# Block-diagonal keys moved by transfers, paired statistics and a 128-row routing product in a fused two-layer attention and feed-forward kernel

## The reference

```python
x = x + tanh(g_xattn[0]) * L0_xattn(layernorm(x), ctx, ctx)      # 32 query heads of 8, 8 key heads
x = x + tanh(g_ffn[0]) * L0_ffn(layernorm(x), ...)               # quantised gated block, hidden 704
x = x + tanh(g_xattn[1]) * L1_xattn(layernorm(x), ctx, ctx)      # 16 query heads of 16, 4 key heads
x = x + tanh(g_ffn[1]) * L1_ffn(layernorm(x), ...)               # 32 experts, the 8 best of each token
```

## Time and profile before

| | us |
|---|---|
| runs shown: median (lowest, highest) | 442.41 (442.10, 442.42) |
| profiled execution, device time | 442.06 |
| its span, first to last instruction | 440.3 |
| TensorE granted clock, mean | 0.984 of full |
| busy: PE / DVE / ACT / POOL | 391.7 / 301.8 / 223.9 / 216.4 |

### The profile page before, as it was taken

The page is one execution under the profiler, slowest core; times in us unless marked ns, Lnnn a source line. Parts: engine busy times, 40 slices in busy tenths (PEclk is TensorE's granted clock), DMA queues, the critical chain, the costliest instruction groups (busy, mean ns, idle before and its releaser), DMA issues.

```text
span 440.3 us, 6773 instructions
## 1 busy us (share of the span) xinstructions
PE 391.7 (89%) x2248; PEld 333.2 (76%) x2248; DVE 301.8 (69%) x603; ACT 223.9 (51%) x446; POOL 216.4 (49%) x234
## 2 busy tenths in 40 slices
PE   0697879897987988979999999999999999999994
PEld 0486778797986987957788887887687777788773
DVE  5486768878766877657678776665867665666664
ACT  2586766575556653535565544444454444444431
POOL 6788976643166533236666253544343344443510
PEclk9998989999999999969999999999999999999999
DMA  5921111000000000031321212223232343333101
GB/s 162 206 71 39 36 37 37 0 2 2 0 1 1 1 2 0 7 102 38 106 63 47 71 44 66 74 71 96 69 88 77 102 122 107 83 97 89 57 0 48
DMA packets 14339, 25.58 MB, mean 58 GB/s; under 512 B 4513, under 2 KB 7201, under 8 KB 14305
## 3 DMA queue, kind: packets, MB, share of 16 engines
q1 hardware_dynamic: 14304, 25.15, 20.1%
HBM read 24.10 MB, written 1.05 MB: 57 GB/s over the span
## 4 chain that ended last, share of the span: by engine, by line
PE 51%; DVE 3%; ACT 1%; issue 1%; DVEq 0%; ACTq 0%
PE bank L1250 15%; PE bank L1252 14%; PE bank L1251 14%; PE bank L1337 2%; PE bank L1149 1%; PE bank L1130 1%; PE bank L1172 1%; PE bank L1110 1%; DVE h_t L980 1%; PE bank L1205 1%; PE bank L1327 0%; ACT ot L623 0%; DVE hl L985 0%; DVE t_t L974 0%; DVE t_t L961 0%
## 5 line engine op out<-in xcount | busy, mean ns | idle before, releaser
L523 POOL TENSOR_TENSOR wl<-wraw,wh 128x768 fp32r<-128x768 f32 x48 | 88.7, 1848 | 109.3 <-DVE hl L985 109.3
L1250 PE MATMUL bank<-xh,wh 128*128 128x512 f32 (+1 forms) x288 | 109.2, 379 | 3.5 <-DVE t_t L961 3.5
L1252 PE MATMUL bank<-xh,wl 128*128 128x512 f32 (+1 forms) x288 | 103.3, 359 | 0.0
L1251 PE MATMUL bank<-xl,wh 128*128 128x512 f32 (+1 forms) x288 | 103.1, 358 | 0.0
L623 ACT ACTIVATE hh<-h_t 128x512 fp32r<-128x512 f32 (+1 forms) x72 | 40.3, 559 | 100.3 <-DVE h_t L980 83.0
L985 DVE TENSOR_TENSOR hl<-h_t,hh 128x512 fp32r<-128x512 f32 (+1 forms) x72 | 49.1, 682 | 24.8 <-ACT hh L623 24.7
L1250 PEld LDWEIGHTS bank<-xh,wh 128*128 128x128 f32 x288 | 55.2, 192 | 11.6 <-issue 3.2
L1252 PEld LDWEIGHTS bank<-xh,wl 128*128 128x128 f32 x288 | 55.0, 191 | 8.1
L961 DVE SCALAR_TENSOR_TENSOR t_t<-s_t,bank 128x512 f32<-128x512 f32 (+1 forms) x72 | 42.9, 595 | 26.3 <-ACT s_t L768 25.9
L1250 PE MATMUL bank<-hh,wh 128*128 128x512 f32 (+1 forms) x144 | 53.2, 370 | 8.4 <-DVE x L996 5.6
L1251 PEld LDWEIGHTS bank<-xl,wh 128*128 128x128 f32 x288 | 55.3, 192 | 7.0
(11 more groups left out here) (105 smaller groups left out, 616.0 us busy)
## 6 DMA issues: line engine op xcount, KB each, us to landing
wraw<-w SPq DMA_DIRECT2D x54, 384.0 KB, 3.1
out<-x SPq DMA_DIRECT2D x8, 128.0 KB, 2.4
x<-x_in SPq DMA_DIRECT2D x1, 768.0 KB, 5.0
ctx_v<-ctx_in SPq DMA_DIRECT2D x2, 256.0 KB, 7.0
ctx_k<-ctx_t SPq DMA_DIRECT2D x2, 192.0 KB, 3.3
x<-x_in SPq DMA_DIRECT2D x1, 256.0 KB, 2.7
wc<-wc_t SPq DMA_DIRECT2D x1, 256.0 KB, 3.9
ot<-sel_in SPq DMA_DIRECT2D x1, 256.0 KB, 5.3
```

What stands on the lines that cost most here:

```text
L523: ops.tensor_tensor(wl[:, slot, :], src, wh[:, slot, :].bitcast(F32), ALU.subtract).then_inc(F.w_split, 1)
L1250: nc.tensor.matmul(o, wh[:, slot, w_sl], rh, start=first, stop=False, skip_group_check=reopened)
L1251: nc.tensor.matmul(o, wh[:, slot, w_sl], rl, start=False, stop=False, skip_group_check=reopened)
L1252: return nc.tensor.matmul(o, wl[:, slot, w_sl], rh, start=False, stop=stop, skip_group_check=reopened)
```

## The change

1. **Keys.** For tiles 3 to 7 of each layer POOL makes no `kbd`. SP copies the diagonal blocks from `khl` (high and low part in one tile) into a slot whose zeros are there already: 16 transfers a tile in layer 0 (8 heads, two halves of the rows; 8 rows by 1 KB each), 8 in layer 1 (16 rows by 1 KB), written in runs of 256 bytes. `kbd`'s two middle dimensions change places for this. SP waits for `kh`, `kl` and the scores of the tile that leaves the slot; PE's `scores` waits for the transfers. In SP's queue a tile's transfers stand ahead of load(3) to load(7); layer 1's tiles 3 to 6 ahead of load(9), its tile 7 ahead of load(20).
2. **Statistics.** In layer 0, `ln_stats` and `power` take tiles in pairs, in the tick u = 1 of each even tile, in place of one tile in each.
3. **Routing.** `sel` and `wts` have 128 rows; rows 64 to 127 are zero (`sel` by its input, 512 KB in place of 256 KB; `wts` by a memset on POOL in step 4, for which `route_high` waits).

```diff
+WHOLE = 3
+def moved(layer, t):
+    at = [k for k in range(WHOLE, TT) if k % RING == t % RING]
+    if layer == 0:
+        return 16 * 16 * (at.index(t) + 1)
+    slot = (TT + t) % RING
+    below = [k for k in range(WHOLE, TT) if k % RING == slot]
+    return 16 * 16 * len(below) + 16 * 8 * (at.index(t) + 1)
...
+        khl = sb("khl", [P, BATCH, 2, KEYS], F32R)
+        kh, kl = khl[:, :, 0], khl[:, :, 1]
...
-        sel_raw = ot[0:2 * EXPERTS].rearrange("p k n -> p (k n)")
-        sel = sb("sel", [2 * EXPERTS, QUADS * P], F32R)
-        wts = sb("wts", [2 * EXPERTS, 2, BLK], F32R)
+        sel_raw = ot[:].rearrange("p k n -> p (k n)")
+        sel = sb("sel", [P, QUADS * P], F32R)
+        wts = sb("wts", [P, 2, BLK], F32R)
...
+            def move_keys(a, t):
+                sp.wait_ge(kh_ready, 2)
+                sp.wait_ge(kl_ready, 3)
+                sp.wait_ge(a.scored, a.units * (t - RING + 1))
+                slot = (a.layer * TT + t) % RING
+                for h in range(a.hk):
+                    for c in range(2):
+                        row = slice(64 * c + h * a.d, 64 * c + (h + 1) * a.d)
+                        sp.dma_start(kbd[row, slot, :, :, h * KEYS:(h + 1) * KEYS]...,
+                                     khl[row, 2 * t:2 * t + 2]...).then_inc(k_moved[slot], 16)
...
+                if WHOLE <= i < TT:
+                    move_keys(A[0], i)
+                if i == F0 + WRAW:
+                    for t in range(WHOLE, TT - 1):
+                        move_keys(A[1], t)
+                if i == 20:
+                    move_keys(A[1], TT - 1)
                 load(i)
...
             def key_part(a, t, r):
+                if t >= WHOLE:
+                    return
...
+                if u == 1 and t % 2 == 0 and t + 2 < TT:
+                    power(a, t + 2, t + 4)
                 if u == 1 and t + 2 < TT:
-                    power(a, t + 2, t + 3)
-                    if n == 9:
-                        pool.wait_ge(kl_ready, 3)
                     key_part(a, t + 2, 1)
...
+                if s == 4:
+                    ops.memset(wts[:].bitcast(F32), 0.0).then_inc(R.wt_zero, 1)
...
-                if u == 1 and t + 2 < TT:
+                if u == 1 and t % 2 == 0 and t + 2 < TT:
...
-                    ln_stats(a, t + 2, t + 3)
+                    ln_stats(a, t + 2, t + 4)
...
-                    if a.layer == 0:
+                    if t >= WHOLE:
+                        pe.wait_ge(k_moved[(a.layer * TT + t) % RING], moved(a.layer, t))
+                    elif a.layer == 0:
```

More of the change, by code:

```diff
@@ L290, in __init__ @@
         self.wt_lo = sem("r_wt_lo")
+        self.wt_zero = sem("r_wt_zero")
         self.sel_loaded = sem("r_sel_loaded")
@@ L315, in build @@
         ctx_k = sb("ctx_k", [P, BATCH, KEYS])
-        kh = sb("kh", [P, BATCH, KEYS], F32R)
-        kl = sb("kl", [P, BATCH, KEYS])
+        khl = sb("khl", [P, BATCH, 2, KEYS], F32R)
+        kh, kl = khl[:, :, 0], khl[:, :, 1]
         ctx_v = sb("ctx_v", [P, BATCH, 64])
@@ L392, in build @@
         kl_ready = sem("kl_ready")
+        k_moved = [sem(f"k_moved{i}") for i in range(RING)]
         v_zeroed = [sem("v_zeroed0"), sem("v_zeroed1")]
@@ L406, in keys @@
             shape = [P, 2, a.hk, KEYS]
-            part = kh[:].bitcast(F32) if r == 0 else kl[:]
+            part = khl[:, :, r].bitcast(F32)
             slot = (a.layer * TT + t) % RING
-            return ops.tensor_tensor(kbd[:, slot, r, :, 0:a.ns].rearrange("p b (h t) -> p b h t", t=KEYS),
+            return ops.tensor_tensor(kbd[:, slot, :, r, 0:a.ns].rearrange("p b (h t) -> p b h t", t=KEYS),
                                      part[:, b, :].unsqueeze(2).to_broadcast(shape),
@@ L437, in _ @@
                              ).then_inc(v_loaded, 16)
+            def move_keys(a, t):
[6 more added lines that the diff above has]
+                        row = slice(64 * c + h * a.d, 64 * c + (h + 1) * a.d)
+                        sp.dma_start(kbd[row, slot, :, :, h * KEYS:(h + 1) * KEYS].rearrange("p b r t -> p (b r) t").bitcast(F32),
+                                     khl[row, 2 * t:2 * t + 2].rearrange("p b r t -> p (b r) t").bitcast(F32)
+                                     ).then_inc(k_moved[slot], 16)
             def load(i):
@@ L799, in route_high @@
                 act.wait_ge(R.wt_done, h + 1)
+                act.wait_ge(R.wt_zero, 1)
                 copy(wts[0:EXPERTS, h, :], bank[PB][0:EXPERTS, :]).then_inc(R.wt_hi, 1)
@@ L1111, in scores @@
                                                 qt[:, t % 2, b2, 2 * gp:2 * gp + 2, :].rearrange("p g s -> p (g s)"),
-                                                kbd[:, slot, r, b2, 0:a.ns], start=(r == 0), stop=(r == 1))
+                                                kbd[:, slot, b2, r, 0:a.ns], start=(r == 0), stop=(r == 1))
                 done.then_inc(a.scored, 1)
@@ L1418 @@
         "kmask1": own_rows(4),
-        "sel_in": np.tile(np.repeat(np.eye(EXPERTS, dtype=np.float32), 32, axis=1), (2, 1)),
+        "sel_in": np.pad(np.tile(np.repeat(np.eye(EXPERTS, dtype=np.float32), 32, axis=1), (2, 1)),
+                         ((0, P - 2 * EXPERTS), (0, 0))),
     }
```

## The result

The changed kernel takes 436.84 us (median of 7 runs, 435.9 to 440.8) against 442.12 for the kernel before: ratio 0.9896 with a 95% interval of 0.9857 to 0.9935, so about 4.6 us faster. Forecast were 428.0 and a range from 422.5 to 435.5. The profiled execution took 436.58 us, its span is 434.5.

The account below looks back on a forecast made before the run. POOL's queue was taken to bound layer 0's attention and PE the experts' stage. 442.06 - 8.8 (keys) - 5.9 (routing) gave 427.4, 427.7 against the median, and 428.0 with 0.3 for layer 1's tile 7; range 422.5 to 435.5 us.

Parts of the forecast that it names:

- What takes POOL's place: SP: SP's queue with the key transfers: 0.6 us an issue, 9.6 us a tile, costing nothing, at most 1 us.
- part 1: Keys moved off POOL in layer 0's attention: 8.8 us gained, with ends of 3 and 11 us.
- Part 3: Routing product padded to 128 rows in the experts' stage: 5.9 us gained on PE, with ends of 0 and 6.4.
- deciding point of 1.1 us: Price per issue on SP up to which tile 3's 16 transfers in layer 0 still arrive before its scores.
- ACT waits for weight blocks 3 to 5: A sign that the prediction is wrong: ACT standing still for these blocks, which SP loads; no size given.
- POOL bounds layer 0's attention: POOL's queue makes its addition to x late there; 4.6 us of PE's idle time come from it.
- slow DVE instruction of 2.10 us: At 82.00 us, beside a POOL key product, where others of its size take 0.43; 1.3 us counted as gained.
- Part 2: Paired statistics in layer 0: some 2 us less on POOL, but no change of the time, within 0.3 us.
- Layer 1's tile 7: Its key transfers stand behind load(19) and end at 249.0, scores at 249.43; 0.3 us of cost allowed.
- SP becomes the bound: Rival: layer 0's 80 transfers make the kernel slower, 452 us at 1.3 us an issue, 500 at 1.9; chance 0.08.
- both effects cancel: Rival: gain and SP's cost balance with issues near 1.15 us, so the time does not change; chance 0.02.
- DVE and ACT as next bound: Rival: these engines hold layer 0's ticks, the moved keys give only 3 us, time 433.5 us; chance 0.14.
- a spread that costs the same: Rival: the routing product costs as much with 128 rows as with 64, time 434 us; chance 0.08.

Follow-up runs that it names:

- e9: The changed kernel with 13 in place of 16 key transfers for each tile of layer 0: 430.92 us, ratio 0.9735 to the kernel before.
- e4: The changed kernel with the routing product back at 64 rows: 443.56 us, ratio 0.9984 to the kernel before.
- e3: The kernel before with the paired statistics alone: 440.89 us, ratio 0.9944.
- e5: The changed kernel with loads ahead of layer 0's key transfers and the routing product at 64 rows: 435.75 us, ratio 0.9831 to the kernel before.
- e8: The changed kernel with POOL making tiles 3 and 4 of both layers and transfers from tile 5 on: 434.03 us, ratio 0.9829 to the kernel before.
- e1: The changed kernel with load(3) to load(7) ahead of layer 0's key transfers in SP's queue: 431.46 us, ratio 0.9744 to the kernel before.
- e6: The changed kernel with loads ahead of layer 0's key transfers and statistics of single tiles: 430.75 us, ratio 0.9721 to the kernel before.
- e2: The kernel before with the 128-row routing product alone: 438.17 us, ratio 0.9895.
- e7: The changed kernel with loads first and 16 more, unused transfers behind each tile's 16 in layer 0: 470.04 us, ratio 1.0603 to the kernel before.

## Why the prediction was wrong

**The step that failed** is "What takes POOL's place: SP", with its "Cost: nothing, with an upper end of 1 us". Its term was mis-sized: 0.60 us an issue, taken from transfers of 64 rows, where the 8-row ones take 0.73. In the sum that is 16 x 0.13 = 2.1 us a tile, and the loads stand behind up to three tiles of it: load(5) came at 62.43 in place of about 56. e9 gives the prediction its own price and lands at 0.9735 against the forecast's 428.0 / 442.4 = 0.967; the rest, 2.9 us, is about what parts 1 and 3 fell short by. The price lay well inside the bounds that I gave it (0.43 to 1.9), but I followed the upper end to the keys alone: tile 3's deadline, hence a deciding point of 1.1 us. load(4) and load(5) are behind the same transfers, and their deadlines moved nearer with the very ticks that part 1 shortens. ACT's timeline in the kernel before has the old deadline of block 5:
```profile
66.67 0.84 ACT L704 ACTIVATE wf<-wraw 128x768 f32<-128x768 int32 x1
```
In the changed kernel block 5 is there at 66.00, in time for the old pace; in e9 ACT takes it at 59.20. So whatever ticks 8 to 15 win, the wait for this block gives back nearly all of it. At 0.73 the two blocks were late by 2.1 and 4.5 us, the clock went to half behind the longer stop, and part 1's 7.5 us were gone (e4). So the range left out a loss that its own bounds contained. That ACT waits for weight blocks 3 to 5 stood among the prediction's signs of being wrong, but no rival gave it a price.

**Point by point.**
- POOL bounds layer 0's attention: right, by e3, e5 and e8. Tick 8's transposes came 2.6 us earlier (38.31 to 35.68; forecast 2.3); 0.4 of it is there before the first key product that falls away (tick 3: 25.43 to 25.04). Until 65 us the clock stayed at full speed, as forecast. The sign that POOL is below 6 tenths from 33 us on was not met: it is at 8 up to 43 us, with work that is no key product.
- Part 1, 8.8 us: 7.5 where no weight block is late (e5, pairs included), with 8.8 inside its interval. Tick 15's transposes, forecast at about 54, are at 54.70 in e1. The slow DVE instruction of 2.10 us takes 0.43 in e1, as counted; but that others of its size take 0.43 was read too simply, since in the kernel before two more took 1.72 (at 65.78) and 1.02 (at 77.84).
- Part 2, nothing: right beside the moved keys (e6), 2.5 us without them (e3).
- Part 3, 5.9 us: 4.6 alone (e2), with 5.9 in its interval; 3.9 by the ratios of the change and e4. The distances fell to 0.23 as forecast; why the kernel gains less than 16 x 0.39 stays open.
- Layer 1's tile 7, 0.3 us: nothing, PE waits for no transfer.
- The rival "SP becomes the bound" had the place right. e7 supports its price (465 forecast, 470.0 measured, with a late block's part in it), but SP decides far earlier than at 1.1 us, through the loads and not through the keys. That both effects cancel came true for keys and pairs (e4), at 0.73 us an issue and not at 1.15.
- The rivals of DVE and ACT as next bound and of a spread that costs the same are excluded by e1 and e2.

The Trainium skill's rule on many small transfers (page "DMA: Bandwidth & Descriptors", section "Rules for kernel authors"), that they be joined into a large one, since under 64 KB one pays mostly overhead, pointed at the right part. The overhead that counted here was the issue, 0.73 us of SP for 8 KB against 0.44 for a weight block of 384 KB in the same rows.

## What to carry to other kernels

When work goes to a queue that is in order, list everything that stands behind it in that queue with the time it is needed, and move those times forward by what the change itself gains. Carry both ends of an unknown price through every one of these deadlines; here 0.13 us an issue decided over 7 us. Put transfers with an early deadline ahead of a long series without one: here the order alone (e1) gave 6.7 us more by the ratios, against 4.6 for the change as it was made.

## What the hardware showed unexpectedly

In these runs an issue on SP costs by the form of the transfer, not by its bytes (e7). In the changed kernel 16 issues of 8 rows take 11.7 us (0.73 each), 8 issues of 16 rows 5.06 (0.63 each), a weight block of 128 rows 0.44 behind a series and 0.33 when SP comes to it from a wait. The timeline of SP in the changed kernel, layer 1's tile 7 and the load behind it:
```profile
241.03 5.06 SPq L462 DMA_DIRECT2D kbd<-khl  x8
246.92 0.33 SPq L470 DMA_DIRECT2D wraw<-w  x1
```
Why fewer rows cost more was not tried. And a matmul's rows matter to its neighbours: around a 64-row product between 128-row ones the distances were 0.39 us longer than around one padded with zeros, and e2's 4.6 us are 0.29 for each of 16. The weight load of 64 rows did not start beside the matmul before it; that of 128 rows does, as the timeline of PEld in the changed kernel shows (the matmul before it starts at 341.05):
```profile
341.06 0.19 PEld L1377 LDWEIGHTS bank<-wts,sel 128*128 128x128 f32 x1
```
e2 shows that the rows are the cause; that they act through the late load is read from these rows alone.
